# A running sum of softmax weights on GpSimd, added in halves of 256 columns instead of whole tiles of 512

## The chip, the core and the metric

The kernel runs on one core of one Trainium2 chip. The metric is the time of one execution on the device in microseconds, the median of several runs. The core has five engines that run side by side, each in its own fixed order: TensorE (PE in the profile, its weight loads PEld), VectorE (DVE), ScalarE (ACT), GpSimd (POOL) and SyncE (SP, which here only issues DMAs). An engine that has to wait for another does so on a semaphore, and everything behind the waiting instruction on that engine waits too.

## What is computed

A cross attention from 16 batches of 128 tokens to 16 contexts of 2048 rows, a chunked delta-rule memory, and a layer of 16 experts. The part that matters here is the attention's softmax:

```python
x = x + xattn(layernorm(x), ctx_1024, ...)          # 16 heads of 32, one shared K and V
#   scores = einsum('bhqd,bkd->bhqk', Q, K) * scale
#   attn   = softmax(scores, axis=-1)
#   out    = einsum('bhqk,bkd->bhqd', attn, V)
x = x + memory(layernorm(x), Ww, Wr, decay, log_alpha)
x = x + experts(layernorm(x), Wg, w1, w2)            # top-1 routing, w1, relu, w2
```

The kernel exponentiates scores tile by tile and keeps the weights unnormalised. For the denominator it adds up the weight tiles, and only at the end sums the result over the 128 partitions and divides.

## The kernel before

**Tiling.** A batch is 64 units: 4 groups of heads (`g`) by 16 blocks of 128 keys (`k`). For each unit TensorE makes scores of 128 keys by 512 (4 heads by 128 tokens) in `score` (L454), ScalarE takes their exponential into one of 18 buffers `p[...]` (`expo_of`, L686), TensorE multiplies the weights by V four units at a time (`weigh`, L466), and GpSimd adds the tile to the group's running sum `psum` in `add_weights` (L1072). The first add of a group takes two weight tiles as inputs, the other 14 take the sum and a tile: 60 adds a batch, 960 in all.

**What sets the order.** Every engine walks the same table of ticks, 128 to a batch, two ticks to a unit. While batch `b` is in its units, the keys, values and queries of batch `b+1` are prepared (`prepare`), the maxima of the next group are taken (`largest`, L441 on TensorE and L864 on VectorE; `turn_max`, L446), and the attention's end, the memory and the routing of batch `b-1` run (`finish`, tick numbers in `POST`). So GpSimd's queue has other things between its adds: three inverse square roots for layer norms (`rsqrt`, L1075, L1077, L1079), the residual and bias adds L1092 and L1098, the low part of the queries L1087, the norms of the memory's keys L1101 and L1103, the identity L1112, and the scatter of the routed rows L1122.

**Who waits for the adds.** Three places wait on the semaphore `psum_pool`, which counts the finished adds: the next add of the same group, since it reads the sum that the last one wrote; `expo_of`, which may overwrite a weight buffer only when the tile of 18 units ago has been added; and `sums` on TensorE at tick 12 of the next batch (L488), which sums the four `psum` tiles over the partitions and needs all 60 adds. After `sums`, VectorE takes reciprocals (L928), TensorE projects (L416 on `wo`), VectorE adds the residual (L938) and takes the statistics (L915, L919), GpSimd takes the inverse root (L1075 to L1079), and ScalarE normalises (L701).

One more line comes up below: L911, VectorE's `kT` low part, a subtraction of 32 by 512 whose two inputs and output all lie in SBUF. It runs four times a batch, at ticks 22, 41, 62 and 78. Most of VectorE's other work reads PSUM.

After attention the experts run on their own, with TensorE the busiest engine.

Of the kernel before, what the change touches and what calls it, by code (L numbers as in the profile page):

```python
# [8 lines left out]
ALU, ACT, AX = mybir.AluOpType, mybir.ActivationFunctionType, mybir.AxisListType  # L9
# [5 lines left out]
KB = S // P  # L15
HG = NH // 4
# [13 lines left out]
UNITS = HG * KB  # L30
NP = 18
# [94 lines left out]
def attention(nc, T, w1_first, w1_in):  # L126
    with ExitStack() as ctx:
# [3 lines left out]
        def count(name, per=1, by=1):  # L131
            return Count(ctx.enter_context(nc.semaphore(name)), per, by)

        def named(name, names):
            return Named(ctx.enter_context(nc.semaphore(name)), names)
# [34 lines left out]
        p = [weights[:, 512 * i:512 * (i + 1)] for i in range(NP)]  # L170
# [46 lines left out]
        a_pe, max_dve, mneg_dve, mrow_act = (  # L217
            count("a_pe", 17 * HG), count("max_dve", UNITS), count("mneg_dve", HG), count("mrow_act", HG))
        b_pe, p_act, pv_pe = count("b_pe", UNITS), count("p_act", UNITS), count("pv_pe", UNITS // 4)
        psum_pool, oS_act, sums_pe = count("psum_pool", HG * (KB - 1)), count("oS_act", HG), count("sums_pe")  # L220
        o_dve = named("o_dve", "recip0 recip1 recip2 recip3 att")


# [52 lines left out]
        def kv_read(b, use):  # L276

            n = kv_uses.index((b, use))
            if n == 0:
                return None  # L280
            before_b, (kind, c) = kv_uses[n - 1]
            if kind == "k":
                return kvs_dve.at(before_b, c)
            return q_dve.at(before_b) if kind == "q" else o_dve.at(before_b, "recip3")
# [15 lines left out]
        def summed(n):  # L300

            g, k = divmod(n, KB)
            return 15 * g + max(k, 1) - 1
# [100 lines left out]
        def _(e):  # L404
# [65 lines left out]
            def busy(n):  # L470

                for _ in range(n):
                    e.matmul(A_BANK[0][0:P - 4, 0:P - 4], mneg[:, 4:P], mneg[:, 4:P], start=True, stop=True)

            def sums(b):

                if b == LAST:
                    e.wait_ge(*mrow_act.at(LAST, HG - 1))
                    busy(8)
                e.wait_ge(*psum_pool.at(b, 15 * HG - 1))  # L480
                e.wait_ge(*oS_act.at(b, HG - 1))
                if b:
                    e.wait_ge(*late_dve.at(b - 1, "ohloc"))
                e.wait_ge(*kv_read(b, ("s", 0)))
                for out, lhs, src in ((KV_BANK, cst[:, C_ONES, 0:HD], [psum[(HG * b + g) % 5] for g in range(HG)]),
                                      (P_BANK, cst[:, C_STACK, 0:HD], oS)):
                    for g in range(HG):
                        ins = e.matmul(out[HD * g:HD * (g + 1), :], lhs, src[g][:], start=True, stop=True)  # L488
                ins.then_inc(sums_pe.sem, 1)
# [153 lines left out]
            for i in range(-2, B + 2):  # L643
                if i == 0:
                    e.wait_ge(*set_dve.at(SET_DVE - 1))
                if i == 1:
                    e.wait_ge(*set_pool.at(SET_POOL - 1))
                    e.wait_ge(*w_in.at(WEIGHTS - 1))
                    e.wait_ge(*const_in.at(CONSTS - 1))
                    e.wait_ge(*dec_dve.at(DEC_DVE - 1))  # L650
                for t in range(TICKS if i <= B else TAIL):
                    if 0 <= i < B and t % 2 == 0:
                        score(i, t // 2)
                    if i == -1 and t in WARM:
                        for _ in range(WARM[t]):
                            e.matmul(P_BANK[:, 0:P], mneg[:], mneg[:], start=True, stop=True)
                    if 0 <= i + 1 < B:
                        prepare(i + 1, t)
                    if i + 2 < B:
                        prepare(i + 2, t - TICKS)  # L660
                    for b, u in quads_in(i, t):
                        weigh(b, u)
                    if 1 <= i <= B and t == POST["sums"]:
                        sums(i - 1)
                    for b, g, n in maxima_in(i, t):
                        largest(b, g, n)
                    for b, g in turns_in(i, t):
                        turn_max(b, g)
                    if i >= 2:
                        finish(i - 2, t + TICKS)  # L670
                    if 1 <= i <= B:
                        finish(i - 1, t)

        @block.scalar
        def _(e):
# [4 lines left out]
            def expo_of(b, u):  # L680
                n = 64 * b + u
                e.wait_ge(*b_pe.at(b, u))
                if n >= NP:
                    e.wait_ge(*pv_pe.at(0, (n - NP) // 4))
                    e.wait_ge(*psum_pool.at(0, summed(n - NP)))
                e.activation(p[n % NP], B_BANK[u % 2][:], ACT.Exp).then_inc(p_act.sem, 1)  # L686

            def max_row(b, g):
# [139 lines left out]
            for i in range(-2, B + 2):  # L828
                for t in range(TICKS if i <= B else TAIL):
                    if 0 <= i < B and t % 2 == 0:  # L830
                        expo_of(i, t // 2)
                    if 0 <= i + 1 < B:
                        prepare(i + 1, t)
                    if i + 2 < B:
                        prepare(i + 2, t - TICKS)
                    done = group_in(i, t, O_COPY)
                    if done:
                        out_sum(*done)
                    for b, g in turns_in(i, t):
                        max_row(b, g)  # L840
                    if i >= 2:
                        finish(i - 2, t + TICKS)
                    if 1 <= i <= B:
                        finish(i - 1, t)
                    if i == 0:
                        once(t)
# [203 lines left out]
        def _(e):  # L1050
# [8 lines left out]
            def add_weights(b, u):  # L1059
                g, k = divmod(u, KB)  # L1060
                if k == 0:
                    return
                e.wait_ge(*p_act.at(b, u))
                acc = psum[(HG * b + g) % 5]
                if k == 1:
                    if HG * b + g >= 5:
                        e.wait_ge(*sums_pe.at((HG * b + g - 5) // HG))
                    first = p[(UNITS * b + u - 1) % NP]
                else:
                    e.wait_ge(*psum_pool.at(b, 15 * g + k - 2))  # L1070
                    first = acc[:]
                e.tensor_tensor(acc[:], first, p[(UNITS * b + u) % NP], ALU.add).then_inc(psum_pool.sem, 1)  # L1072

            def rsqrt(mv, rs, b, done, tag):
                e.tensor_tensor(rs[:, 0:1], mv[:, 1:2], eps[:, 0:1], ALU.add).then_inc(done.sem, 1)  # L1075
# [50 lines left out]
            for i in range(-2, B + 2):  # L1126
                if i == 1:
                    e.wait_ge(*w_in.at(WEIGHTS - 1))
                    e.wait_ge(*zeroed.at(ZEROES - 1))
                for t in range(TICKS if i <= B else TAIL):  # L1130
                    if 0 <= i < B and t % 2:
                        add_weights(i, t // 2)
                    if 0 <= i + 1 < B:
                        prepare(i + 1, t)
                    if i + 2 < B:
                        prepare(i + 2, t - TICKS)
                    if i >= 2:
                        finish(i - 2, t + TICKS)
                    if 1 <= i <= B:
                        finish(i - 1, t)  # L1140
# [196 lines left out]
def program(nc, T):  # L1337
    with ExitStack() as ctx:
        w1_first = ctx.enter_context(nc.sbuf_tensor("w1_first", [P, DC, F], F32))
        w1_in = [Count(ctx.enter_context(nc.semaphore(f"w1_in0{j}")), 1, 16) for j in range(2)]  # L1340
        attention(nc, T, w1_first, w1_in)
        experts(nc, T, w1_first, w1_in)
# [51 lines left out]
```

## Time and profile before

| | us |
|---|---|
| median of 3 runs (2177.47, 2177.59, 2180.35) | 2177.59 |
| the profiled execution | 2181.67 |
| its span in the profile | 2179.8 |
| attention, up to GpSimd's last add | 1690.8 |
| one batch in the steady part (between last adds) | 102.8 |
| TensorE busy over the span | 2101.6 (96%) |
| GpSimd busy over the span | 1636.3 (75%) |

The profile is one execution. A row of its timeline has the start, the time taken, the engine, the line in the kernel, the operation with output and inputs, how many like instructions were merged, and in brackets the idle time ahead with what ended it. Gaps of at most 0.15 us are not told of in brackets and merged rows run over them, so a merged row of several adds holds the gaps between them too. A wait is put down to whoever came last by the profile.

### The profile page before, as it was taken

Reading aid. Unit: us, or ns where it says so; the run is one execution under the profiler, and the core shown is the slowest. Engines: PE = TensorE matmul, PEld = TensorE weight load, DVE = VectorE, ACT = ScalarE, POOL = GpSimd, SP = SyncE. Lnnn points to the kernel's source line nnn. Section 1 sums busy time; section 2 is a strip of 40 time slices with the busy share of each in tenths; the row PEclk is TensorE's granted clock in tenths of the full one; section 3 lists DMA queues with packets and bytes.
Section 4 is the critical chain, followed back from the end, with each engine's and each line's share of the span. In section 5 each row is a group of like instructions: output and inputs, shape, how many; then the busy total and the mean of one; then the engine's idle time right before and its main releaser. Section 6 shows DMA issues by size and latency. Waiting matters only on the chain. (4 is left out here: it accounts for less than half of the span.)

```text
span 2179.8 us, 35745 instructions
## 1 busy us (share of the span) xinstructions
PE 2101.6 (96%) x12908; PEld 1428.9 (66%) x12908; DVE 1277.2 (59%) x2226; ACT 1220.5 (56%) x2277; POOL 1636.3 (75%) x1387
## 2 busy tenths in 40 slices
PE   8879999999999999999999999999989989999999
PEld 5436565656565656666565656565645889999998
DVE  5656767676666666676767676666664433333333
ACT  3656575666666566666665666666655223333333
POOL 0788888888888888888888888889798145555555
PEclk8999999999999999999999999999999999999999
DMA  4752121212212121212131212112200089999994
GB/s 160 233 119 89 48 74 44 73 52 66 75 48 74 45 73 54 73 43 82 39 96 42 74 43 73 60 56 71 79 15 11 12 302 355 363 345 366 360 349 177
DMA packets 107056, 262.31 MB, mean 120 GB/s; under 512 B 8961, under 2 KB 34305, under 8 KB 98689
## 3 DMA queue, kind: packets, MB, share of 16 engines
q1 hardware_dynamic: 96912, 234.92, 31.6%
q10 hardware_dynamic: 6384, 14.62, 2.4%
q0 software_dynamic: 3584, 10.49, 1.2%
q8 instruction: 103, 1.69, 0.3%
q14 instruction: 73, 0.59, 0.1%
HBM read 223.67 MB, written 25.72 MB: 114 GB/s over the span
## 5 line engine op out<-in xcount | busy, mean ns | idle before, releaser
L1072 POOL TENSOR_TENSOR psum<-psum,weights 128x512 f32<-128x512 f32 x896 | 1153.1, 1287 | 161.1 <-ACT weights L686 57.3
L864 DVE TENSOR_REDUCE mpart<-bank 128x1 f32<-128x512 f32 x1024 | 680.1, 684 | 304.8 <-PE bank L441 296.5
L686 ACT ACTIVATE weights<-bank 128x512 f32<-128x512 f32 x1024 | 596.9, 599 | 330.3 <-PE bank L454 324.9
L454 PE MATMUL bank<-qT,kT 97*128 97x512 f32 x1024 | 482.3, 477 | 13.2 <-DMA qT<-mrow 10.2
L441 PE MATMUL bank<-kT,qT 96*128 96x512 f32 x1024 | 449.9, 451 | 8.1 <-DVE mpart L864 5.4
L441 PEld LDWEIGHTS bank<-kT,qT 96*128 96x128 f32 x1024 | 196.8, 192 | 138.8 <-issue 88.7
L1324 POOL TENSOR_TENSOR w2l<-w,w2h 128x1024 fp32r<-128x1024 f32 x64 | 202.9, 3171 | 77.1 <-PE ebank L1237 56.0
L454 PEld LDWEIGHTS bank<-qT,kT 97*128 97x128 f32 x1024 | 195.9, 193 | 90.4 <-issue 48.6
L466 PE MATMUL bank<-weights,v 128*32 128x512 f32 x2048 | 251.9, 610 | 0.0
L721 ACT COPY w_first<-bank 128x512 f32<-128x512 f32 x248 | 144.7, 584 | 65.1 <-PE bank L412 62.2
L1267 ACT ACTIVATE hh<-ebank 128x512 fp32r<-128x512 f32 x64 | 38.2, 597 | 225.7 <-PE ebank L1221 225.7
L412 PE MATMUL bank<-cst,w_first 128*128 128x128 f32 x992 | 151.0, 275 | 7.4 <-ACT w_first L721 4.7
L412 PEld LDWEIGHTS bank<-cst,w_first 128*128 128x128 f32 x992 | 119.7, 141 | 50.8 <-issue 20.4
L1261 ACT CAST w2h<-w 128x2048 fp32r<-128x2048 f32 x64 | 121.4, 1898 | 44.1 <-DMA w<-in_w 44.1
L466 PEld LDWEIGHTS bank<-weights,v 128*32 128x32 f32 x2048 | 54.0, 110 | 122.1 <-issue 92.4
L532 PE MATMUL bank<-w_first,wkv 128*64 128x512 f32 x512 | 125.4, 611 | 0.0
L1293 DVE SCALAR_TENSOR_TENSOR hl<-ebank,hh 128x512 fp32r<-128x512 f32 x64 | 44.2, 691 | 133.9 <-ACT hh L1267 133.9
L1288 DVE TENSOR_TENSOR w2l<-w,w2h 128x1024 fp32r<-128x1024 f32 x64 | 79.3, 1239 | 73.2 <-PE ebank L1237 49.4
L1221 PE MATMUL ebank<-dT,w_first 128*128 128x128 f32 x1024 | 118.5, 275 | 0.9 <-DVE dT L1282 0.9
L1221 PEld LDWEIGHTS ebank<-dT,w_first 128*128 128x128 f32 x1024 | 117.7, 192 | 2.4 <-issue 1.1
L1221 PEld LDWEIGHTS ebank<-dT,w 128*128 128x128 f32 x1024 | 117.5, 192 | 1.4
L1221 PE MATMUL ebank<-dT,w 128*128 128x128 f32 x1024 | 118.2, 275 | 0.0
(169 smaller groups left out, 3053.5 us busy)
## 6 DMA issues: line engine op xcount, KB each, us to landing
w<-in_w SPq DMA_DIRECT2D x48, 2048.0 KB, 20.2
w_first<-in_ctx SPq DMA_DIRECT2D x62, 1024.0 KB, 5.1
w_first<-in_w SPq DMA_DIRECT2D x16, 2048.0 KB, 12.7
dispatched<-route ACTq DMA_DIRECT2D x17, 513.0 KB, 10.3
dis<-dispatched SPq DMA_DIRECT2D x16, 513.0 KB, 3.5
qT<-qh SPq DMA_DIRECT2D x128, 64.0 KB, 3.4
qT<-qs SPq DMA_DIRECT2D x64, 64.0 KB, 2.1
xr<-in_x SPq DMA_DIRECT2D x16, 256.0 KB, 2.7
```

Of the source, the lines that this page charges most:

```text
L412: ins = e.transpose(out[0:m, j * P:(j + 1) * P], src(j), ident)
L441: e.matmul(a[:], qT[b % 2][0:3 * HD, (4 * g + h) * P:(4 * g + h + 1) * P], kT[b % 2][0:3 * HD, c * 512:(c + 1) * 512], start=True, stop=Tr ...
L454: e.matmul(B_BANK[u % 2][:], kT[b % 2][0:3 * HD + 1, k * P:(k + 1) * P], qT[b % 2][0:3 * HD + 1, g * 512:(g + 1) * 512], start=True, stop= ...
L466: ins = e.matmul(PV_BANK[HD * j:HD * (j + 1), :], v1[b % 2][:, k + j, :], p[(UNITS * b + u + j) % NP], start=k == 0, stop=k == KB - 4)
L532: ins = e.matmul(KV_BANK[rows, :], wkv[:, j, :], cxT[c % 2][:, j, :], start=j < 2, stop=j >= 2)
L686: e.activation(p[n % NP], B_BANK[u % 2][:], ACT.Exp).then_inc(p_act.sem, 1)
L721: e.copy(cxT[c % 2][:, :, kk * P:(kk + 1) * P], turn_bank(b, ("t", k))[:].rearrange("p (c t) -> p c t", c=DC)).then_inc(cxT_act.sem, 1)
L864: e.tensor_reduce(mpart[g % 2][:, 4 * (n % 4) + n // 4:4 * (n % 4) + n // 4 + 1], max_bank(b, g, n)[:], AX.X, ALU.max).then_inc(max_dve.se ...
L1072: e.tensor_tensor(acc[:], first, p[(UNITS * b + u) % NP], ALU.add).then_inc(psum_pool.sem, 1)
L1221: ins = e.matmul(H_BANK[g][:, f * P:(f + 1) * P], w1[q][:, c, (4 * g + f) * P:(4 * g + f + 1) * P], dT[q][:, c, :], start=c == 0, stop=c = ...
L1261: e.copy(w2h[g][:], w2[q][:, 4 * g:4 * g + 4, :]).then_inc(w2h_act.sem, 1)
L1324: e.tensor_tensor(w2l[g % 2][:, 2:4, :], w2[q][:, 4 * g + 2:4 * g + 4, :], w2h[g][:, 2:4, :].bitcast(F32), ALU.subtract).then_inc(w2l_pool ...
```

## The change

`add_weights` issues two instructions a unit in place of one, each on 256 of the 512 columns, and each raises `psum_pool` by one. A half waits for the same half of the unit before, not for all of it. The three waits count in halves accordingly: `sums` waits for all 120 of a batch, and `expo_of` for the second half of the unit that read its buffer.

```diff
-        psum_pool, oS_act, sums_pe = count("psum_pool", HG * (KB - 1)), count("oS_act", HG), count("sums_pe")
+        psum_pool, oS_act, sums_pe = count("psum_pool", 2 * HG * (KB - 1)), count("oS_act", HG), count("sums_pe")
...
-                e.wait_ge(*psum_pool.at(b, 15 * HG - 1))
+                e.wait_ge(*psum_pool.at(b, 2 * 15 * HG - 1))
...
-                    e.wait_ge(*psum_pool.at(0, summed(n - NP)))
+                    e.wait_ge(*psum_pool.at(0, 2 * summed(n - NP) + 1))
...
-                    e.wait_ge(*psum_pool.at(b, 15 * g + k - 2))
                     first = acc[:]
-                e.tensor_tensor(acc[:], first, p[(UNITS * b + u) % NP], ALU.add).then_inc(psum_pool.sem, 1)
+
+                for half in range(2):
+                    cols = slice(256 * half, 256 * (half + 1))
+                    if k > 1:
+                        e.wait_ge(*psum_pool.at(b, 2 * (15 * g + k - 2) + half))
+                    e.tensor_tensor(acc[:, cols], first[:, cols], p[(UNITS * b + u) % NP][:, cols], ALU.add).then_inc(
+                        psum_pool.sem, 1)
```

Nothing moves on the other engines. On GpSimd, this is its queue before, around the turn from one batch to the next, down to the inverse root of the second layer norm (`sums_pe` is the signal of `sums`, `p_act` that of the exponentials):

```order
L1072 TENSOR_TENSOR psum<-weights 128x512 [waits sums_pe,p_act]
L1092 TENSOR_TENSOR xr<-xr,bo 128x512 [waits xr_in]
L1072 TENSOR_TENSOR psum<-psum,weights 128x512 [waits psum_pool,p_act] x2
L1119 TENSOR_TENSOR before<-before,oh 128x16 [waits late_pe]
L1121 TENSOR_TENSOR pad_pool<-mhalf 128x1 [waits late_dve]
L1122 DMA dispatched<-route,sidx 2176x1026
L1072 TENSOR_TENSOR psum<-psum,weights 128x512 [waits psum_pool,p_act] x7
L1075 TENSOR_TENSOR rs<-mv,eps 128x1 [waits post_dve]
```

And this is the same stretch of GpSimd's queue in the changed kernel, whose lines from the add on are numbered 4 or 5 higher; left out are further pairs like the two rows above each gap:

```order
L1076 TENSOR_TENSOR psum<-weights 128x256 [waits sums_pe,p_act]
L1076 TENSOR_TENSOR psum<-weights 128x256
L1097 TENSOR_TENSOR xr<-xr,bo 128x512 [waits xr_in]
L1076 TENSOR_TENSOR psum<-psum,weights 128x256 [waits psum_pool,p_act]
L1076 TENSOR_TENSOR psum<-psum,weights 128x256 [waits psum_pool]
...
L1124 TENSOR_TENSOR before<-before,oh 128x16 [waits late_pe]
L1126 TENSOR_TENSOR pad_pool<-mhalf 128x1 [waits late_dve]
L1127 DMA dispatched<-route,sidx 2176x1026
...
L1080 TENSOR_TENSOR rs<-mv,eps 128x1 [waits post_dve]
```

Each add has become a pair in the same place; the first half of a pair takes the wait for the exponential, and both halves wait for their own column range of the unit before.

## Rows read from the trace of the kernel before

**Rows 1.** The profile's first part: busy us, share of the span, instructions.

```profile
PE 2101.6 (96%) x12908; PEld 1428.9 (66%) x12908; DVE 1277.2 (59%) x2226; ACT 1220.5 (56%) x2277; POOL 1636.3 (75%) x1387
```

**Rows 2.** One steady batch: length, busy us (instructions) by engine, clock, DMA.

```profile
877.00:979.90 102.90, 101.17 (x610) 62.82 (x608) 69.47 (x125) 66.23 (x134) 87.58 (x82) 1.00 0.21 61
```

**Rows 3.** TensorE's longest wait in that batch: us in total, times, longest.

```profile
PE bank L446 <- DVE mneg L871: 0.8, 1, 0.8
```

**Rows 4.** GpSimd's groups by shape, whole run: count, busy us, mean ns, idle before.

```profile
L1072 POOL TENSOR_TENSOR psum<-psum,weights 128x512 f32<-128x512 f32 x896 | 1153.1, 1287 | 161.1 <-ACT weights L686 57.3 <-POOL psum L1072 1.3
L1119 POOL TENSOR_TENSOR before<-before,oh 128x16 f32<-128x16 f32 x16 | 3.5, 221 | 6.2 <-PE bank L638 6.2
```

**Rows 5.** Durations of two lines, ns: least, median, most.

```profile
L1072 POOL TENSOR_TENSOR psum<-psum,weights x896: 1259/1276/1666, 55.1 to 1689.6; 128x512 f32<-128x512 f32 x180
L911 DVE TENSOR_TENSOR kT<-kvs,kT x64: 680/682/1648, 17.6 to 1558.5; 32x512 fp32r<-32x512 f32 x64
```

**Rows 6.** GpSimd's timeline in that batch and into the next.

```profile
905.28 1.04 POOL L1103 TENSOR_TENSOR rn<-rn,mhalf 128x4 f32<-128x4 f32 x1
...
914.65 1.28 POOL L1112 TENSOR_TENSOR xr<-xr,cst 128x512 f32<-128x512 f32 x1 [1.15 <-DVE xr L944]
915.89 12.61 POOL L1072 TENSOR_TENSOR psum<-psum,weights 128x512 f32<-128x512 f32 x9
...
967.61 0.19 POOL L1075 TENSOR_TENSOR rs<-mv,eps 128x1 f32<-128x1 f32 x1 [0.30 <-DVE rs L919]
...
968.66 11.23 POOL L1072 TENSOR_TENSOR psum<-psum,weights 128x512 f32<-128x512 f32 x8
979.85 1.28 POOL L1072 TENSOR_TENSOR psum<-weights 128x512 f32<-128x512 f32 x1
981.09 1.28 POOL L1092 TENSOR_TENSOR xr<-xr,bo 128x512 f32<-128x512 f32 x1
982.33 2.69 POOL L1072 TENSOR_TENSOR psum<-psum,weights 128x512 f32<-128x512 f32 x2
...
986.66 10.02 POOL L1072 TENSOR_TENSOR psum<-psum,weights 128x512 f32<-128x512 f32 x7
997.48 0.19 POOL L1075 TENSOR_TENSOR rs<-mv,eps 128x1 f32<-128x1 f32 x1 [0.80 <-DVE rs L919]
```

**Rows 7.** TensorE's timeline where `sums` starts.

```profile
980.64 0.60 PE L412 MATMUL bank<-cst,w_first 128*128 128x128 f32 x4
981.17 1.07 PE L488 MATMUL bank<-psum,cst 128*32 128x512 f32 x8
```

**Rows 8.** ScalarE's timeline at the keys' norms and, a batch on, the second layer norm.

```profile
906.98 1.27 ACT L759 ACTIVATE rk<-xn,rn 128x128 f32<-128x128 f32 x4
...
998.62 0.81 ACT L701 ACTIVATE xn<-x,rs 128x512 f32<-128x512 f32 x1 [0.94 <-POOL rs L1079]
...
1000.01 0.60 ACT L686 ACTIVATE weights<-bank 128x512 f32<-128x512 f32 x1
```

**Rows 9.** VectorE's timeline at two of L911's four places.

```profile
910.08 0.85 DVE L911 TENSOR_TENSOR kT<-kvs,kT 32x512 fp32r<-32x512 f32 x1
...
994.49 1.05 DVE L911 TENSOR_TENSOR kT<-kvs,kT 32x512 fp32r<-32x512 f32 x1 [0.57 <-ACT kT L735]
995.57 0.69 DVE L938 TENSOR_TENSOR x<-bank,xr 128x512 f32<-128x512 f32 x1
```

**Rows 10.** Timelines at the experts' start, GpSimd's row and VectorE's.

```profile
1765.84 6.65 POOL L1324 TENSOR_TENSOR w2l<-w,w2h 128x1024 fp32r<-128x1024 f32 x2 [12.49 <-ACT w2h L1261]
1765.72 1.22 DVE L1288 TENSOR_TENSOR w2l<-w,w2h 128x1024 fp32r<-128x1024 f32 x1 [6.84 <-ACT w2h L1261]
...
1768.01 2.23 DVE L1288 TENSOR_TENSOR w2l<-w,w2h 128x1024 fp32r<-128x1024 f32 x1 [0.46 <-ACT w2h L1261]
```

**Rows 11.** The attention's end: GpSimd's last adds, TensorE's last `sums`.

```profile
1683.92 6.90 POOL L1072 TENSOR_TENSOR psum<-psum,weights 128x512 f32<-128x512 f32 x5
1691.13 1.07 PE L488 MATMUL bank<-psum,cst 128*32 128x512 f32 x8
```

## The prediction

> **What bounds the kernel now.** I read the busy times first: TensorE is busy 96% of the span and GpSimd 75% [rows 1]. An average hides stages, so next one batch of the steady part, cut out by its times: TensorE is busy 101.17 of 102.9 us at full clock, GpSimd 87.58 [rows 2]. So TensorE has 1.7 us a batch to give back, and its longest wait there, 0.8 us, is for VectorE [rows 3]. GpSimd matters only where somebody stands and waits for it, which its timeline shows. It runs to 0.80 us of idle time before L1075, where it waits for VectorE's statistics, and it idled 0.30 us for the same reason before the L1075 of the third norm, 30 us earlier [rows 6]. Between these two it works its queue off without waiting for anybody's data. TensorE's `sums` begins at 981.17 while the 60th add ended at 968.66 + 11.23 = 979.89; TensorE was at other work until then, so that add has 1.28 us to spare [rows 6, 7]. ScalarE does wait, 0.94 us before L701, for L1079 [rows 8], but L1079 is late because L1075 waited for VectorE, not because of the adds.
>
> **What a pair costs.** A whole add takes 1276 ns [rows 5]. Nine chained adds took 12.61 us, so one starts (12.61 - 1.28) / 8 = 1.417 us after the other: the wait for the sum that the last one wrote leaves GpSimd idle 0.14 us [rows 6]. Adds with nothing to wait for start 1.24 us apart, as 979.85 and 981.09 do: a follower starts 0.04 us before its predecessor's end [rows 6]. The trace has no add of 256 columns. The nearest on either side are 221 ns for 16 columns and 1276 for 512 [rows 4, 5], which gives 221 + 240 x (1276 - 221) / 496 = 731 ns. At the least a half costs half of the whole, 638, at the most as much as a whole, 1276; I take 731, since the cost per column between the two rows has no reason to bend. A half's own-signal wait asks for a result that was finished a whole half earlier, 0.69 us, against the 0.14 that a signal takes to be seen, so it should cost nothing, and a half starts 0.69 us after the half before. **A pair is 1.38 us.** That is 0.037 less than a chained add and 0.14 more than one that waited for nothing.
>
> The rule that could speak against this is in the Trainium skill, GPSIMD Engine Reference, "Instruction dispatch": every instruction pays a software dispatch anew. The same page's table gives 4497 ns for an add of 2048 columns; with our 1276 at 512 an estimate from it is 1276 - 256 x (4497 - 1276) / 1536 = 739 ns for a half and 1.40 for a pair, so that by the page the sum below would read the same. No row here has an add of 2048 columns.
>
> **Where it falls.** A run of n adds between other instructions took (n - 1) x 1.417 + 1.24 and will take n x 1.38. From 967.61 to the next batch's 997.48 the runs are 8, 1, 2 and 7 [rows 6]: -0.12, +0.14, +0.10, -0.08, together +0.04 us. GpSimd idles 0.80 us at the end of it, which hides that. Turned round: the 18 adds would have to cost (0.80 - 0.04) / 18 = 0.042 us more each, a pair 1.42, before L1075 is late and ScalarE behind it; that is a half of 751 ns, and each 10 ns beyond it would cost up to 18 x 0.02 = 0.36 us a batch, 5 us in all. The 60th add ends about 0.1 us earlier, into its 1.28 us of room: nothing. The other takers: the keys' norm L1103 ends at 906.32 and is used at 906.98, with runs of 2 and 3 adds in the queue since the root, +0.10 and +0.07 against 0.66 of room [rows 6, 8]; before L1112 GpSimd idles 1.15 us [rows 6], against +0.14 for a lone add. ScalarE's waits for free weight buffers look 18 units back, 18 x 1.6 = 29 us, and GpSimd has caught up with its work at each of the idle times above. The added instructions ride on GpSimd's queue alone, and 221 ns [rows 4] is all that a whole instruction of 16 columns takes, so issuing twice as many is no limit at one per 690 ns. Sum over the steady batches: 0.
>
> **At the attention's end** TensorE has little else. The last add ends at 1683.92 + 6.90 = 1690.82 and `sums` starts at 1691.13 [rows 11]. The last 15 adds there stand in the queue as runs of 7 and 8 with the third norm between, -0.08 and -0.12, so `sums` may start up to 0.2 us earlier. The experts are untouched and only shift.
>
> **VectorE's side.** L911 has both inputs in SBUF. It takes 680 to 1648 ns [rows 5], 1.05 of them ahead of the second norm, and L938 starts right behind it [rows 9]. Adds reach 1666 ns. Both fit one cause: GpSimd and such an instruction take turns, VectorE waiting for the end of the add and the next add for VectorE. The Trainium skill names it in GPSIMD Engine Reference, "Specifications": GpSimd's SBUF interfaces are shared with VectorE, with contention when VectorE reads two SBUF inputs; the spread of these rows agrees. If VectorE gets its turn at an instruction's end, halves offer one every 0.69 us rather than 1.42, and L911 ends between 0.37 us earlier (1.05 - 0.68) and, with a half just begun, some 0.2 us later. Earlier brings the norm forward, where TensorE has no idle time to fill; I count it as 0. What if VectorE needs GpSimd to be idle? Today each chained add leaves 0.14 us for that, the halves leave none. The one row against it: at 1766 two L1324 ran back to back, 6.65 us, and the L1288 that started at 1768.01 was through after 2.23 us, against 1.22 for the one before it [rows 10]. It ended at 1770.24, while GpSimd was busy until 1772.49. So a turn is given at the boundary.
>
> **The sum.** Against the profiled execution's own 2181.67: 0 for the batches, -0.2 at the end, 2181.5. The median of the three runs is 4.1 lower than that execution; applied to it, 2177.59 - 0.2 = **2177.4 us**. A measurement of this kernel can tell about 0.2%, 4.4 us, from no change.
>
> **Rivals.**
> *Starved VectorE (slower).* L911 gets no turn while halves follow without a gap. Ahead of the second norm it would wait until GpSimd runs dry at about 996.7, end at 997.3 rather than 995.54, and take L938, L1075, L701 and the exponentials behind with it: 1.7 us. At tick 41 it began at 910.08 and would wait until the idle time before L1112, from 913.5 on, and end some 3 us late; TensorE's maxima wait behind it. Up to 4.7 us x 15 turns of a batch, of which TensorE may catch up some: 60 us, or **2237**. It decides if a back-to-back boundary gives VectorE nothing; for it speaks that nearly all contested boundaries of the trace had the 0.14 us gap, against it the row at 1768. Chance 5%.
>
> *The halves don't overlap (slower).* Each half starts at the end of the one before: a pair is 1.46. 18 x (1.46 - 1.38) = 1.44 us, less 0.76 of room, leaves 0.7 us a batch at L1075, 15 x 0.7 = 10 us, **2188**. A half of 770 ns without any of that would cost the same. Against it are all unchained followers, which start 0.04 us early. 6%.
>
> *The signal waits don't go away.* Then the change doesn't do what it says: each half pays 0.14, a pair is 2 x (0.73 + 0.14) = 1.74. GpSimd needs 60 x 1.74 + 10.8 for the rest (87.58 less 60 adds of 1.28) = 115 us a batch, more than 102.9; 15 x 12.3 = 184, **2362**. It would take a signal over 0.69 us to be seen; rows show 0.14. 2%.
>
> *VectorE is freed and TensorE profits (faster).* L911's 0.37 us there and 0.17 at tick 41 come off every batch: 15 x 0.54 = 8 us, **2169.5**. For it: VectorE's chain leads to L701, ahead of exponentials that TensorE needs (0.94 us of idle, [rows 8]). Against it: TensorE's waits in the batch are elsewhere [rows 3], and it is busy 98% already. 10%.
>
> *The forecast.* Nothing but up to 0.2 us at the end: 77%. It may be off by the spread of the three runs, about 3 us.
>
> **Numbers.** The range leaves out starvation, lost signals, most of the 2188 case and most of the faster one: 2173 to 2186. Its upper end is a half of about 767 ns, its lower the faster rival at half its size. Faster by over 0.2%: 10%. Within: 77%. Slower: 5 + 6 + 2 = 13%.
>
> **What would show it.** In the changed kernel: halves of about 731 ns, a merged run of 14 halves near 14 x 0.69 = 9.7 us; 0.5 to 1.1 us of idle time left before L1080; batches of 102.8 us; `sums` at least 1 us behind the last half; L911 at most about 1.3 us. A half over 0.75 us, or L911 waiting through several halves, would make the prediction wrong on the slow side; batches under 102.5 us on the fast side.

## The result, and the profile after

| | before | after |
|---|---|---|
| median | 2177.53 us (4 runs) | 2235.77 us (2234.01 to 2240.13, 4 runs) |
| profiled span | 2179.8 | 2238.3 |
| last add ends | 1690.8 | 1749.1 |
| one steady batch | 102.8 | 105.3 to 108.2 |

The changed kernel takes 1.0262 times as long (95% interval 1.025 to 1.0274). All 58 us are lost before the last add: 1749.1 against 1690.8. The experts only shift.

The page's first part and its group for the second and later halves, to be read against [rows 1] and [rows 4]:

```profile
PE 2131.4 (95%) x12908; PEld 1441.0 (64%) x12908; DVE 1336.5 (60%) x2226; ACT 1222.4 (55%) x2277; POOL 1743.8 (78%) x2347
...
L1076 POOL TENSOR_TENSOR psum<-psum,weights 128x256 f32<-128x256 f32 x1792 | 1252.2, 733 | 86.8 <-ACT weights L686 86.2
```

A half costs 733 ns on average, so the size is as forecast. GpSimd isn't late either: it works 1743.8 us of 2238.3. Two other numbers grew: VectorE by 59 us (1277.2 to 1336.5) at the same 2226 instructions, and TensorE by 30. VectorE has no new work, so some instruction of it takes longer. Grouped by tile, the one that does in nearly every batch is L1004, a `scalar_tensor_tensor` of 128 by 1 that adds up three columns of `sc` into the scatter index `sidx`, once a batch, at tick 8 of the next one. Its durations are in ns: least, median, most; first the changed kernel, then the one before.

```profile
L1004 DVE SCALAR_TENSOR_TENSOR sidx<-sc x16: 219/4616/4644, 260.9 to 1806.6; 128x1 uint32<-128x1 f32 x16
```

```profile
L1004 DVE SCALAR_TENSOR_TENSOR sidx<-sc x16: 220/624/1001, 261.0 to 1748.2; 128x1 uint32<-128x1 f32 x16
```

An instruction of 128 numbers takes 4.6 us. The timelines around it show what it stood beside and who stood behind it. Columns are as in [rows 6]; first VectorE, then GpSimd, then TensorE, in the changed kernel at the turn of a batch.

```profile
1007.80 4.60 DVE L1004 SCALAR_TENSOR_TENSOR sidx<-sc 128x1 uint32<-128x1 f32 x1
...
1012.63 0.68 DVE L864 TENSOR_REDUCE mpart<-bank 128x1 f32<-128x512 f32 x1
```

```profile
995.78 0.20 POOL L1084 TENSOR_TENSOR rs<-rs 128x1 f32<-128x1 f32 x1
995.93 11.09 POOL L1076 TENSOR_TENSOR psum<-psum,weights 128x256 f32<-128x256 f32 x16
1006.97 1.43 POOL L1076 TENSOR_TENSOR psum<-weights 128x256 f32<-128x256 f32 x2
1008.35 1.29 POOL L1097 TENSOR_TENSOR xr<-xr,bo 128x512 f32<-128x512 f32 x1
1009.59 2.78 POOL L1076 TENSOR_TENSOR psum<-psum,weights 128x256 f32<-128x256 f32 x4
1012.33 0.22 POOL L1124 TENSOR_TENSOR before<-before,oh 128x16 f32<-128x16 f32 x1
...
1014.47 8.25 POOL L1076 TENSOR_TENSOR psum<-psum,weights 128x256 f32<-128x256 f32 x12
...
1028.34 0.19 POOL L1080 TENSOR_TENSOR rs<-mv,eps 128x1 f32<-128x1 f32 x1 [2.48 <-DVE rs L919]
```

```profile
1010.30 0.66 PE L412 MATMUL bank<-cst,w_first 128*128 128x128 f32 x4
1013.36 0.79 PE L441 MATMUL bank<-kT,qT 96*128 96x512 f32 x1 [2.40 <-DVE mpart L864]
```

Each GpSimd row starts at or just before the end of the one ahead, from 995.93 to 1012.33: 23 wide instructions with no gap. L1004 arrives at 1007.80, in the 18th of them, and ends at 1012.40, with the last. Five instruction boundaries passed it by. Behind it on VectorE stand the maxima L864 (here at 1012.63), and TensorE's `largest` waits 2.40 us for them. Summed over the run, TensorE's wait for those grew from 5.4 us to this (total us, times, longest):

```profile
PE bank L441 <- DVE mpart L864: 43.4, 22, 4.3
```

The longest, 4.3 us, is in the first batch and stands behind another instruction: L911, which the prediction had looked at, took 6.00 us there instead of 0.68, beside a run of 18 halves. It came in the 11th of them, and it ended 0.54 us after the last.

```profile
117.51 6.00 DVE L911 TENSOR_TENSOR kT<-kvs,kT 32x512 fp32r<-32x512 f32 x1
```

The stop costs more than itself. The windows below are of TensorE alone: length, busy us (instructions), granted clock, then DMA.

```profile
1012.00:1013.00 1.00, 0.00 (x0) 1.00 0.03 8
1013.00:1014.00 1.00, 0.64 (x2) 0.67 0.00 0
1014.00:1015.00 1.00, 1.00 (x5) 0.50 0.00 0
1015.00:1016.00 1.00, 1.00 (x5) 0.50 1.02 406
1016.00:1017.00 1.00, 1.00 (x9) 0.62 0.97 156
1017.00:1018.00 1.00, 1.00 (x16) 1.00 0.83 164
```

After the 2.40 us of idling the granted clock falls to 0.50, the 1.2 GHz level, for some 3.4 us, and half of that, 1.7 us, is lost again. It isn't so after every stop. In the 13 steady batches, from 260.1 to 1648.3, the stop is the same 2.4 us (2.39 to 2.45), but behind three of the 13 the clock stays at 1.00, behind six it is at 0.50 for some 3.4 us, and behind four for some 6.8. One batch of each kind, in the columns of [rows 2]:

```profile
686.90:792.20 105.30, 101.30 (x609) 62.91 (x608) 73.05 (x125) 66.10 (x134) 94.19 (x142) 1.00 0.20 61
580.30:686.90 106.60, 102.61 (x609) 63.76 (x608) 73.22 (x125) 66.26 (x134) 94.18 (x141) 0.98 0.20 60
792.20:900.30 108.10, 104.13 (x609) 63.99 (x609) 73.25 (x125) 66.31 (x134) 94.17 (x142) 0.97 0.20 60
```

TensorE is busy 0.1, 1.4 and 3.0 us longer than the 101.17 of [rows 2], with the same matmuls. The stop and the clock together give the batches' 2.5, 3.8 and 5.3 us. Most of TensorE's 30 us of additional busy time are from there. Over the whole run the mean granted clock is 0.973, against 0.987 before. Why equal stops were followed by 0, 3.4 or 6.8 us at the lower clock stays open.

### The profile page after: what moved, and what is told of

Same layout as the page of the kernel before. It is cut to its first block and busy times, and to the rows that moved or that the text cites. A ratio compares the mean times of both kernels' runs of the same rounds, so it can differ in the third digit from the quotient of the medians.

```text
span 2238.3 us, 36705 instructions
## 1 busy us (share of the span) xinstructions
PE 2131.4 (95%) x12908; PEld 1441.0 (64%) x12908; DVE 1336.5 (60%) x2226; ACT 1222.4 (55%) x2277; POOL 1743.8 (78%) x2347
## 5 line engine op out<-in xcount | busy, mean ns | idle before, releaser
L1076 POOL TENSOR_TENSOR psum<-psum,weights 128x256 f32<-128x256 f32 x1792 | 1252.2, 733 | 86.8 <-ACT weights L686 86.2
L864 DVE TENSOR_REDUCE mpart<-bank 128x1 f32<-128x512 f32 x1024 | 681.6, 684 | 315.0 <-PE bank L441 306.8
L441 PE MATMUL bank<-kT,qT 96*128 96x512 f32 x1024 | 456.7, 457 | 46.1 <-DVE mpart L864 43.4
L454 PE MATMUL bank<-qT,kT 97*128 97x512 f32 x1024 | 488.3, 483 | 6.1 <-DMA qT<-mrow 3.0
L466 PE MATMUL bank<-weights,v 128*32 128x512 f32 x2048 | 265.7, 639 | 0.0
L1076 POOL TENSOR_TENSOR psum<-weights 128x256 f32<-128x256 f32 x128 | 90.8, 731 | 43.7 <-ACT weights L686 43.7
```

The lines of the kernel that those rows point to most:

```text
L441: e.matmul(a[:], qT[b % 2][0:3 * HD, (4 * g + h) * P:(4 * g + h + 1) * P], kT[b % 2][0:3 * HD, c * 512:(c + 1) * 512], start=True, stop=Tr ...
L454: e.matmul(B_BANK[u % 2][:], kT[b % 2][0:3 * HD + 1, k * P:(k + 1) * P], qT[b % 2][0:3 * HD + 1, g * 512:(g + 1) * 512], start=True, stop= ...
L466: ins = e.matmul(PV_BANK[HD * j:HD * (j + 1), :], v1[b % 2][:, k + j, :], p[(UNITS * b + u + j) % NP], start=k == 0, stop=k == KB - 4)
L864: e.tensor_reduce(mpart[g % 2][:, 4 * (n % 4) + n // 4:4 * (n % 4) + n // 4 + 1], max_bank(b, g, n)[:], AX.X, ALU.max).then_inc(max_dve.se ...
L1076: e.tensor_tensor(acc[:, cols], first[:, cols], p[(UNITS * b + u) % NP][:, cols], ALU.add).then_inc(psum_pool.sem, 1)
```

## The experiments

The theory at this point: halves leave GpSimd no gap, and without a gap a VectorE instruction with two SBUF inputs gets no turn. Open were the cause (gap or width), whether L1004 is all of it, and what the rule is, since [rows 10] showed a turn given without a gap.

### Is it L1004, and its two inputs?

The same sum written with two per-partition scalars has one tensor input. It was put into the changed kernel and into the one before.

```diff
-                    e.scalar_tensor_tensor(sidx[:], sc[:, 6:7], sc[:, 4:5], sc[:, 5:6], ALU.add, ALU.add).then_inc(
+                    e.tensor_scalar(sidx[:], sc[:, 6:7], sc[:, 4:5], sc[:, 5:6], ALU.add, ALU.add).then_inc(
```

> The changed kernel, with one of VectorE's instructions in another form: L1004 (sidx, 128x1) becomes a tensor_scalar with both summands as per-partition scalars, so it has one tensor input from SBUF and not two; the result is the same. Theory A (VectorE's instructions with two SBUF tensor inputs find no turn beside back-to-back halves, and L1004, 4.6 us in place of 0.62, is where the time went): L1004 falls to about 0.15-0.25 us, TensorE's 2.4 us wait for mpart goes, batches are 102.8 us and the time is 2177 +- 5 us. Theory B (the halves cost in GpSimd's own queue, or by their number of instructions and signals, and L1004's length is only a symptom): it stays at 2225 to 2240.

> The kernel before, with the same other form of L1004. Control for e1. Theory A: L1004 falls from 0.62 to about 0.2 us, nothing waits for that, 2177 +- 3. Theory B: the same. Should it be clearly faster (under 2173), the instruction cost time already beside whole adds.

In the kernel before: 2179.63 us, ratio 1.0001 (0.9991 to 1.0011), nothing, as expected. In the changed kernel: 2191.57, ratio 1.0061 (1.0045 to 1.0078). That is 44 of the 58 us, a miss of 14. L1004 itself is cured (first row), but now the first of a batch's four L911, at tick 22, waits (second and third row: VectorE, then GpSimd beside it):

```profile
L1004 DVE TENSOR_SCALAR sidx<-sc x16: 272/273/275, 257.5 to 1756.6; 128x1 uint32<-128x1 f32 x16
```

```profile
997.50 2.45 DVE L911 TENSOR_TENSOR kT<-kvs,kT 32x512 fp32r<-32x512 f32 x1 [0.57 <-ACT kT L735]
```

```profile
989.77 9.63 POOL L1076 TENSOR_TENSOR psum<-psum,weights 128x256 f32<-128x256 f32 x14
1001.89 0.19 POOL L1080 TENSOR_TENSOR rs<-mv,eps 128x1 f32<-128x1 f32 x1 [2.48 <-DVE rs L919]
```

L911 comes in the 12th half, is refused at the boundaries that follow, and finishes at 999.95, just after GpSimd has run dry at 999.40 and stands at L1080 for the statistics behind that very L911. This is the starvation that the prediction described at this place, 1.8 us of it; the 2.45 us are 1.4 more than the 1.05 of [rows 9]. In the changed kernel's steady batches it didn't show: the stop behind L1004 had left GpSimd without tiles (1.72 us of idle time before its row at 1024.45), so that its run was only two halves old when L911 came at 1025.54, and L911 took 0.86. One delay hid the other. Only ahead of the first L1004, at 260.88, did L911 wait long: the 6.00 us shown above, and 2.16 at 171.42.

### Does every short run refuse a turn?

A kernel of its own, with nothing of the problem computed: GpSimd does 14 adds, and one instruction of VectorE is sent in after 3 of them, at four different offsets into an add. The adds are whole or half, free of waits, chained one to the next, or in pairs as in the change.

> A measurement by itself, not the problem's computation (all of that is left out): GpSimd issues 14 adds, VectorE meanwhile one probe, 72 times. Adds: whole or half width, free (no wait), chained (each waits for the one before), in pairs (each waits for the one two before, like the change). Probes: the scalar_tensor_tensor of L1004's form (128x1, two SBUF tensors), the subtraction of L911's form (32x512, two SBUF tensors), the tensor_scalar with two per-partition scalars (128x1). Theory A1: with chained adds a two-input probe takes at most one add more than alone (about 1.3 or 0.75 us), with free and paired adds it waits for the end of the run, 4 to 13 us; the tensor_scalar never waits, about 0.15 to 0.25 us. Theory A2: whole adds give a turn at each boundary whether chained or not, halves do not. A forecast turn at every boundary, as in the prediction, would show at most one add's wait in all rows.

```profile
L86 DVE SCALAR_TENSOR_TENSOR half_pair_stt<-c x4: 210/387/570, 569.7 to 599.7; 128x1 uint32<-128x1 f32 x4
L86 DVE SCALAR_TENSOR_TENSOR whole_free_stt<-c x4: 727/926/1111, 11.6 to 64.2; 128x1 uint32<-128x1 f32 x4
L90 DVE TENSOR_SCALAR half_pair_ptr<-c x4: 264/266/267, 650.4 to 680.3; 128x1 uint32<-128x1 f32 x4
```

Each was given a turn at the next boundary, gap or no gap, half or whole: the spread of 360 ns is the offset into the add. Both versions of the theory failed. The form with one tensor input waits for nothing (264 to 267 ns). The Trainium skill says in "SBUF — State Buffer", "Who interferes with whom", that a VectorE instruction with at most one SBUF input, outside VectorE's 2-port modes, does not contend with GpSimd and one with two does; these rows and L1004's 273 ns agree.

### Is it the length of the run?

What differed between this and the kernel was how many instructions had already followed one another. The adds became 28, and the instruction was sent in after 1, 4, 7, 10, 13, 16, 20 or 24 of them (A to H).

> A measurement by itself (the problem's computation is left out). GpSimd issues 28 adds in a row, VectorE one probe with two SBUF inputs after 1, 4, 7, 10, 13, 16, 20 or 24 of them (marks A to H): the scalar_tensor_tensor of 128x1, or a subtraction of 32x64. Adds: halves in pairs as in the change (own signal two back), the same with a second, satisfied wait on every other one, free halves, whole adds in pairs, chained halves. Theory C (a turn needs all of GpSimd at a boundary at once, and its eight cores drift apart the longer instructions follow each other without a gap; this case's traces give turns after 0 to 5 such instructions and refuse them after 10 or more): with halves in pairs and free ones the probe waits at most one half (under 0.9 us) at A, B, C and for the rest of the run (3 us and more) from D or E on; chained ones never over 0.9 us. Theory D (the length of the run does not matter; the refusal comes from something else in the kernel, two waits on an instruction or the traffic of other engines): every probe under one add plus 0.25 us, or only the two-wait rows are long.

```profile
L88 DVE SCALAR_TENSOR_TENSOR half_pair_stt_after_E<-c x1: 520/520/520, 100.7 to 100.7; 128x1 uint32<-128x1 f32 x1
L88 DVE SCALAR_TENSOR_TENSOR half_pair_stt_after_F<-c x1: 8000/8000/8000, 122.1 to 122.1; 128x1 uint32<-128x1 f32 x1
L88 DVE SCALAR_TENSOR_TENSOR half_pair_stt_after_H<-c x1: 2561/2561/2561, 166.5 to 166.5; 128x1 uint32<-128x1 f32 x1
L88 DVE SCALAR_TENSOR_TENSOR whole_pair_stt_after_E<-c x1: 1058/1058/1058, 789.5 to 789.5; 128x1 uint32<-128x1 f32 x1
L88 DVE SCALAR_TENSOR_TENSOR whole_pair_stt_after_F<-c x1: 14460/14460/14460, 827.6 to 827.6; 128x1 uint32<-128x1 f32 x1
L88 DVE SCALAR_TENSOR_TENSOR half_chain_stt_after_F<-c x1: 641/641/641, 1313.5 to 1313.5; 128x1 uint32<-128x1 f32 x1
```

That is it. After 13 adds the turn is given in 0.52 us; after 16 it takes 8.00, which is the rest of the run (12 adds at 0.68), and after 24 it takes 2.56, again the rest. Whole adds behave alike, at 14.46 us, so between 256 and 512 columns width plays no part; the halves only doubled the number. Free halves, halves of which every other one has a second wait that is met long before, and a subtraction of 32 by 64 in L1004's place change at the same letter (8.00, 8.00 and 8.06 us at F). Chained halves, each of which waits for the one before and so leaves a gap (22.32 us for 28 instead of 19.08, 0.12 each), give the turn always.

### What is the length measured in, and does other load move it?

The same with 24 adds, the instruction sent in after 4, 6, 8, 10, 12, 13, 14, 15 or 16 (A to I).

> A kernel of its own with nothing of the problem in it: 24 adds of 256 columns on GpSimd without a gap, and VectorE's scalar_tensor_tensor of 128 by 1 issued after 4, 6, 8, 10, 12, 13, 14, 15 or 16 of them (letters A to I of the tiles' names). The last experiment put the number of back-to-back GpSimd instructions after which VectorE gets no turn between 13 and 16, while the changed kernel refused it at 11 and 12. Theory C (the length of the gapless run decides) has to say what the length is measured in. If it is a number of instructions: quiet changes from about 0.5 us to over 5 us at one letter among F to I, narrow (32 columns, a third of the time each) changes at the same letter, and mixed (every third add 512 wide) too. If it is time (some 9 to 11 us): narrow never changes (24 narrow adds take under 7 us) and mixed changes earlier, after 8 or 10. reset (a wait for the add before, ahead of the tenth add) has to be given a turn at every letter, since no run is then longer than 15. If it is load from other engines that lowers the number in the kernel: act (ScalarE copies beside it), dma (loads beside it) or all change earlier than quiet, by letter D or E.

```profile
L97 DVE SCALAR_TENSOR_TENSOR quiet_G<-c x1: 661/661/661, 121.9 to 121.9; 128x1 uint32<-128x1 f32 x1
L97 DVE SCALAR_TENSOR_TENSOR quiet_H<-c x1: 6100/6100/6100, 139.2 to 139.2; 128x1 uint32<-128x1 f32 x1
L97 DVE SCALAR_TENSOR_TENSOR narrow_I<-c x1: 278/278/278, 208.6 to 208.6; 128x1 uint32<-128x1 f32 x1
L97 DVE SCALAR_TENSOR_TENSOR reset_I<-c x1: 660/660/660, 355.8 to 355.8; 128x1 uint32<-128x1 f32 x1
L97 DVE SCALAR_TENSOR_TENSOR mixed_G<-c x1: 664/664/664, 499.6 to 499.6; 128x1 uint32<-128x1 f32 x1
L97 DVE SCALAR_TENSOR_TENSOR mixed_H<-c x1: 7718/7718/7718, 521.2 to 521.2; 128x1 uint32<-128x1 f32 x1
L97 DVE SCALAR_TENSOR_TENSOR act_E<-c x1: 667/667/667, 625.4 to 625.4; 128x1 uint32<-128x1 f32 x1
L97 DVE SCALAR_TENSOR_TENSOR act_F<-c x1: 7485/7485/7485, 642.8 to 642.8; 128x1 uint32<-128x1 f32 x1
L97 DVE SCALAR_TENSOR_TENSOR dma_G<-c x1: 661/661/661, 810.5 to 810.5; 128x1 uint32<-128x1 f32 x1
```

Quiet, the turn is given after 14 adds and refused after 15. With every third add whole the run up to that point takes about a quarter longer, and the letter is the same: it is a number of instructions, not a time. One gap, of 0.08 us ahead of the tenth add, keeps the turn open to the last letter. With ScalarE's copies beside it the turn is given after 12 adds and refused after 13; loads do not move it; with both it is given after 13 and refused after 14. Each letter was measured once. Adds of 32 columns never refused a turn, up to 16 of them, against what the count alone says; they end within 0.21 us of each other, and the 0.40 us at most is one or two of them. So what counts here are wide instructions; more than 16 narrow ones were not tried. This also fits L1004, which got through when the narrow L1124 (128 by 16) came up at 1012.33, with no gap ahead of it.

### Does a gap cure the changed kernel?

The two real kernels refused earlier than the bare one. With ScalarE's copies the bare kernel still gave the turn after 12; the changed kernel refused it when 10 halves were done (L911 at 117.51, with 3.82 us of idle time ahead of the run), and the one-input kernel when 11 were. It isn't a fixed number there either: at 102.83 the one-input kernel gave L911 its turn after 14 halves, in 1.11 us, and the changed kernel did so at 105.03. Other VectorE instructions with two SBUF inputs had just had turns in that run, and its 16 halves took 12.04 us instead of 11.09. Whether a turn given starts the count anew was not tried.

Three ways to put gaps back, all by the index that the first half waits for: the whole unit before instead of its own half. First in every unit.

```diff
-                        e.wait_ge(*psum_pool.at(b, 2 * (15 * g + k - 2) + half))
+                        e.wait_ge(*psum_pool.at(b, 2 * (15 * g + k - 2) + 1))
```

> The changed kernel, but the first half of every unit waits for both halves of the unit before: two instructions a unit, no overlap from unit to unit. A unit costs GpSimd 0.69 + 0.73 + 0.14 = 1.56 us, 60 x 1.56 + 10.8 = 104.4 us a batch, more than the 102.8 that a batch takes. Theory C: no refused turns, L1004 under 1 us, but GpSimd becomes the bound or late at L1075: batches of 104 to 106 us, 2195-2225. Theory D: worse than the changed kernel, over 2236.

2240.65 us, ratio 1.0272 (1.0255 to 1.0289): as slow as the change, for another reason, and above the 2195 to 2225 expected. Nobody is starved (first two rows), but 16 halves now take 12.36 us, 1.55 a pair against 1.38, and GpSimd becomes the bound: its 60 pairs and the 10.8 us of other work are 104 us a batch. A steady batch measures 106.3, of which GpSimd waits only 1.8 for exponentials. TensorE waits for exponentials whose buffers are not yet free, and for the last adds.

```profile
L1004 DVE SCALAR_TENSOR_TENSOR sidx<-sc x16: 219/367/643, 261.4 to 1807.8; 128x1 uint32<-128x1 f32 x16
L911 DVE TENSOR_TENSOR kT<-kvs,kT x64: 680/891/1259, 16.9 to 1605.4; 32x512 fp32r<-32x512 f32 x64
```

```profile
995.74 12.36 POOL L1076 TENSOR_TENSOR psum<-psum,weights 128x256 f32<-128x256 f32 x16
```

```profile
PE bank L454 <- ACT weights L686: 23.4, 17, 4.8
...
PE bank L488 <- POOL psum L1076: 8.6, 14, 3.8
```

Then at four units of each group, so that no more than ten halves follow without a gap, once alone and once with the one-input L1004.

```diff
-                        e.wait_ge(*psum_pool.at(b, 2 * (15 * g + k - 2) + half))
+                        e.wait_ge(*psum_pool.at(b, 2 * (15 * g + k - 2) + (1 if k in (3, 8, 13, 15) else half)))
```

> The changed kernel, but in 4 of 15 units of a group (k = 3, 8, 13, 15) the first half waits for both halves of the unit before, which gives GpSimd 0.14 us of idle time there, at a cost of 0.18 us for such a unit. Theory C: both L1004 and L911 get their turn within two halves, L1004 under 1.3 us, and the time comes back to 2177-2184, as GpSimd's pairs cost 1.43 us on average. Theory D (halves as such, their number or width): L1004 stays over 3 us, 2225-2240.

> e6 with L1004 in the one-input form of e1 as well. Theory C: 2176-2182, within 0.3% of the kernel before, no better, since TensorE is the bound and GpSimd had 0.8 us to spare. Theory D: like e1, about 2191, since L911 would still be refused.

2181.59 us, ratio 1.0007 (0.9997 to 1.0016), and 2181.51, ratio 1.0007 (0.9997 to 1.0017). The loss is gone with 16 gaps a batch, with L1004 as it was and all 120 halves in place:

```profile
L1004 DVE SCALAR_TENSOR_TENSOR sidx<-sc x16: 222/290/495, 256.6 to 1744.4; 128x1 uint32<-128x1 f32 x16
L911 DVE TENSOR_TENSOR kT<-kvs,kT x64: 681/682/1245, 17.4 to 1554.1; 32x512 fp32r<-32x512 f32 x64
```

Then a single gap a batch, at the last unit (g 3, k 15), a little ahead of L1004.

```diff
-                        e.wait_ge(*psum_pool.at(b, 2 * (15 * g + k - 2) + half))
+                        e.wait_ge(*psum_pool.at(b, 2 * (15 * g + k - 2) + (1 if (g, k) == (3, 15) else half)))
```

> The changed kernel with one gap a batch put back: only the first half of the last unit of a batch (g 3, k 15) waits for the whole unit before, a little ahead of L1004. Theory C: the run of gapless instructions ahead of L1004 is then 5 to 8 long, so L1004 gets its turn within one half (0.2 to 0.7 us instead of 4.6). L911 at tick 22 has no gap nearer than in the kernel with the one-input L1004, where VectorE was just as early, so it is refused as there (about 2.4 us in each batch), and the time is that kernel's: 2191, between 2187 and 2196. The rival, that the damage of halves is a matter of their whole density and not of the one run in progress: a single gap a batch changes little, 2225 to 2236. If one gap cures all: 2177 to 2183, and L911 under 1.3 us.

2194.42 us, ratio 1.0069 (1.0056 to 1.0083), between the bounds given, near the 2191.57 of the one-input kernel. One wait of 0.14 us a batch takes back 41 us. L1004 gets through in 0.80, just above the 0.7 expected, in a run that is two halves old and not 5 to 8. L911 is refused as in that kernel, and in the first batch for 5.58 us:

```profile
985.16 0.80 DVE L1004 SCALAR_TENSOR_TENSOR sidx<-sc 128x1 uint32<-128x1 f32 x1
...
999.15 2.62 DVE L911 TENSOR_TENSOR kT<-kvs,kT 32x512 fp32r<-32x512 f32 x1 [0.57 <-ACT kT L735]
```

### Whole adds without gaps

The kernel before, but with even and odd units in two running sums that are added at a group's end, and one weight buffer fewer to make room.

```diff
-                acc = psum[(HG * b + g) % 5]
+                acc = (psum[(HG * b + g) % 5], psum_odd)[k % 2]
...
+                if k == 15:
+                    acc = psum[(HG * b + g) % 5]
+                    e.wait_ge(*psum_pool.at(b, 15 * g + 13))
+                    e.tensor_tensor(acc[:], acc[:], psum_odd[:], ALU.add).then_inc(psum_pool.sem, 1)
```

> The kernel before with whole adds of 512 columns, but two running sums in turn (even and odd units, added together at the group's end), so that no add waits for the one just before it: the 0.14 us of idle time between adds goes while their width stays. 17 weight buffers instead of 18 make room. Theory A1 (what counts is that GpSimd has no idle time between instructions): L1004 is starved, 2 us or more, and the time rises to 2200-2240. Theory A2 (what counts is the half's width or that there are two to a unit): L1004 stays under 1.3 us and the time is 2175 +- 5.

2179.06 us, ratio 0.9996 (0.9987 to 1.0006), with L1004 (L1005 in that kernel) at 731 ns at most: not the 2200 to 2240 of the theory of gaps. It was meant to separate gap from width and did not: the final add waits, so each group has a gap at its end, and L1004 comes right behind that of the last group, when the new run is only a few instructions old. The bare kernel's whole adds (14.46 us) decide that question.

## Why the prediction was wrong

**What bounds the kernel** was read rightly: TensorE, with GpSimd mattering where somebody stands behind it.

**What a pair costs** held: 731 ns forecast, 729 median; 12 halves in a row took 8.25 us, 0.69 each; the signal waits cost nothing, and the halves overlap. The rivals of no overlap and of lost signals fell.

**Where it falls and the attention's end**, 0 and -0.2 us, were sums over GpSimd's own queue. Their terms were right, and GpSimd before L1080 still had idle time, 2.48 us in the batch shown, waiting for VectorE. The 58 us came from none of them: the prediction's term for VectorE's side, 0, was really 2.4 us of stopped TensorE a batch and up to 3.4 us more through its clock.

**"So a turn is given at the boundary"** is the step that failed. It rested on one row, the L1288 of [rows 10], which had met a run of two instructions. The statement is true of short runs, up to 14 instructions in the bare kernel, and was carried over to runs of two dozen. The text before it had the right suspicion: each chained add leaves 0.14 us, the halves leave none. The old waits were taken for a pure cost; they were what kept VectorE's turns coming. The observation that nearly all contested boundaries had such a gap should have weighed more than one row without, because the change abolishes exactly that; a chance of 5% was far too low.

**The victim** was incomplete too. Only L911 was looked for. L1004 is of the same kind, two tensors in SBUF, and before the change its 220 to 1001 ns for 128 numbers told so. It looked harmless for its size, yet the wait doesn't depend on size, and behind it stood `largest`'s maxima.

**The starved rival's 2237** is the time that came, but only half for its reasons. Its 1.7 us for L911 ahead of the second norm is near what the one-input kernel shows (2.45 us instead of 1.05, so 1.4), and there it gave 12 us of loss in all; its 3 us at tick 41 didn't occur (0.89 us at 1016.78 in the one-input kernel, where GpSimd's run was five halves old). The other 44 us came through L1004: 2.4 us of stop in each batch, and behind 10 of the 13 steady ones another 1.7 or 3.4 through the clock, which no term had. That the sums met is chance.

## What to carry to other kernels

Before taking gaps out of GpSimd's queue, list every VectorE instruction with two SBUF inputs, however small, and count the GpSimd instructions since the last gap at the places where they come: ten or more wide ones without a gap, and VectorE may stand until the run ends. A wait on a result of its own that costs GpSimd 0.1 to 0.2 us every ten instructions is then worth keeping, and where VectorE's instruction can be written with one tensor input and per-partition scalars, that is free (2179.63 against 2179.55 in the kernel before). A stall of VectorE is then to be priced by who waits behind it, TensorE's clock included.

## What the runs showed of the hardware

- VectorE instructions with two SBUF inputs take turns with GpSimd at instruction boundaries, but only while GpSimd's gapless run is short: given after 14 adds of 256 columns, refused after 15 (after 13 with ScalarE busy beside it), and in the real kernels refused in the 11th and 12th half, though at 105.03 the changed kernel gave it after 14. Then nothing is given until the run ends: 8.00 us for halves, 14.46 for whole adds, 4.6 and once 6.00 in the kernel. A gap of 0.08 us starts the count anew. Adds of 32 columns never refused, up to 16 of them. VectorE's L1004 with one tensor input and per-partition scalars took 273 ns in the middle of a run of 23.
- The Trainium skill says in "SBUF — State Buffer", "Summary: rules for kernel authors", that the second one to issue blocks until the first finishes. The short runs agree; in the long ones the first had finished many times over.
- Why a count matters was not tried. One candidate is in "GPSIMD Engine Reference", "Instruction dispatch" of the Trainium skill: each of GpSimd's cores starts the next instruction as soon as its own share is done, so that cores could drift apart until there is no moment at which all are between two instructions, and a wait on a result would bring them together again. Nothing here shows the cores, so this stays open, as does what lowers the number in the real kernel.
- After 13 stops of 2.4 us, equal to 0.06 us, TensorE's granted clock stayed at 1.00 three times, stood at 0.50 for about 3.4 us six times and for about 6.8 us four times. Shorter stops in the kernel before, of 0.8 us, left it at 1.00 ([rows 2, 3]).
